# LSTM attention: the softmax numerators turned by four 32-column products with 8 identity columns, in place of one 128x128 transpose

## The reference

```python
def attend(h):
    q = h @ Wq.T
    scores = jnp.einsum('bc,bsc->bs', q, context)
    alpha = jax.nn.softmax(scores, axis=-1)
    ctx = jnp.einsum('bs,bsc->bc', alpha, context)
    return jnp.tanh(jnp.concatenate([ctx, h], axis=-1) @ Wout.T + b_out)

def step(carry, x_t):
    h, c, attn = carry
    inp = jnp.concatenate([x_t, attn], axis=-1)
    gates = inp @ W_ih.T + b_ih + h @ W_hh.T + b_hh
    i, f, g, o = jnp.split(gates, 4, axis=-1)
    c = jax.nn.sigmoid(f) * c + jax.nn.sigmoid(i) * jnp.tanh(g)
    h = jax.nn.sigmoid(o) * jnp.tanh(c)
    out = attn_out = attend(h)
    return ((h, c, attn_out), out)
```

## Time and profile before

| | |
|---|---|
| three timed runs | 6492.47, 6497.38, 6498.66 us; median 6497.38 |
| the profiled execution, its own time | 6499.01 us |
| its span, first to last instruction | 6497.2 us |
| mean granted TensorE clock | 0.966 of full |
| PE busy, share of the span | 89% |
| DVE, ACT busy | 58%, 33% |
| the LSTM loop, first to last transpose on PE | 261.7 to 4528.6 us |

### The profile page before, as it was taken

One profiled execution on the slowest core, in us unless ns is written; L12 is line 12 of the kernel. 1 busy time (PEld: TensorE's weight loads), 2 busy tenths in 40 slices (PEclk: granted clock), 3 DMA queues, 4 the chain that ended last, 5 costly groups with the idle time before them and its releaser, 6 DMA issues. The chain is left out here.

```text
span 6497.2 us, 369971 instructions
## 1 busy us (share of the span) xinstructions
PE 5781.7 (89%) x163920; PEld 3976.9 (61%) x163920; DVE 3736.9 (58%) x16359; ACT 2118.1 (33%) x7992; POOL 290.1 (4%) x779
## 2 busy tenths in 40 slices
PE   6899999999999999999999999999888779795979
PEld 2577777777777777777777777776434334443433
DVE  4355555555555555555555555555387998888852
ACT  3133333333333333333333333333122122222221
POOL 0000000000000000000000000000011011111000
PEclk8999999999999999999999999999898889897989
DMA  1100000000000000000000000000111101010111
GB/s 65 53 2 2 2 2 2 2 2 2 2 2 2 2 2 2 2 2 2 2 2 2 2 2 2 2 2 18 59 39 35 34 21 48 24 55 17 43 31 55
DMA packets 42841, 105.28 MB, mean 16 GB/s; under 512 B 7912, under 2 KB 9960, under 8 KB 42240
## 3 DMA queue, kind: packets, MB, share of 16 engines
q1 hardware_dynamic: 41312, 103.13, 5.2%
q10 hardware_dynamic: 1440, 1.06, 0.1%
HBM read 93.64 MB, written 10.52 MB: 16 GB/s over the span
## 5 line engine op out<-in xcount | busy, mean ns | idle before, releaser
L653 PE MATMUL lstm_part_ps<-lstm_keys,lstm_hid 128*4 128x128 f32 x32768 | 1036.1, 273 | 205.6 <-DVE lstm_hid L804 205.6
L669 PE MATMUL lstm_ctx_ps<-lstm_values,lstm_alpha 128*4 128x128 f32 (+1 forms) x49152 | 1092.6, 237 | 0.0
L653 PEld LDWEIGHTS lstm_part_ps<-lstm_keys,lstm_hid 128*4 128x4 f32 x32768 | 770.4, 86 | 440.2 <-DVE lstm_hid L804 426.0
L669 PEld LDWEIGHTS lstm_ctx_ps<-lstm_values,lstm_alpha 128*4 128x4 f32 x49152 | 895.8, 87 | 94.0
L831 DVE TENSOR_REDUCE lstm_neg_max<-lstm_part_ps 128x1 f32<-128x128 f32 x1024 | 298.4, 291 | 566.3 <-PE lstm_part_ps L653 566.3
L769 ACT ACTIVATE lstm_expo<-lstm_part_ps,lstm_neg_max 128x128 f32<-128x128 f32 x1024 | 376.4, 368 | 749.3 <-DVE lstm_neg_max L831 749.3
L612 PE MATMUL lstm_half_ps<-lstm_w_hid,lstm_hid 128*13 128x96 f32 x16384 | 591.0, 247 | 0.0
L789 DVE STREAM_TRANSPOSE lstm_gates<-lstm_half_ps 128x96 f32<-128x96 f32 x1024 | 289.9, 283 | 433.6 <-PE lstm_half_ps L612 409.5
L612 PE MATMUL lstm_half_ps<-lstm_w_attn,lstm_attn 128*13 128x96 f32 x16416 | 475.5, 247 | 0.7 <-ACT lstm_attn L782 0.7
L776 ACT ACTIVATE lstm_out_row<-lstm_ctx_ps,lstm_factor 128x128 f32<-128x128 f32 x512 | 188.4, 368 | 682.4 <-PE lstm_ctx_ps L669 682.4
L810 DVE COPY lstm_alpha<-lstm_part_ps 128x8 f32<-128x8 f32 x1024 | 176.6, 172 | 382.5 <-PE lstm_part_ps L676 382.5
(11 more groups left out here) (332 smaller groups left out, 8597.5 us busy)
## 6 DMA issues: line engine op xcount, KB each, us to landing
mix_ring<-in_sm_chunks SPq DMA_DIRECT2D x120, 358.0 KB, 3.0
mix_ring<-in_mix_chunks SPq DMA_DIRECT2D x64, 384.0 KB, 3.1
lstm_xg<-xg_rows SPq DMA_DIRECT2D x514, 16.0 KB
xg_rows<-lstm_xg_tile SPq DMA_DIRECT2D x16, 512.0 KB, 2.6
ctxT<-in_ctxT SPq DMA_DIRECT2D x1, 2048.0 KB, 14.8
out_xT<-xT SPq DMA_DIRECT2D x4, 512.0 KB, 3.8
xT<-in_xT SPq DMA_DIRECT2D x1, 1536.0 KB, 9.8
lstm_w_x<-in_lstm_w_x SPq DMA_DIRECT2D x1, 1024.0 KB, 7.8
```

What stands on the lines that cost most here:

```text
L653: mm = pe.matmul(part_rows(score_ps[part], b), hid[:, k, lo:lo + SPACE], keys[:, k, b * SRC + c * P:b * SRC + (c + 1) * P], start=(n == 0 ...
L669: mm = pe.matmul(part_rows(ctx_ps[n], b), alpha[:, b, c, SPACE - 1 - c:2 * SPACE - 1 - c], values[:, b * SC + c, ctx_cols[n]], start=(c == ...
```

## The change

`turn(part)` no longer transposes 128x128. It issues four products, one for each group of 32 positions: the stationary operand is `expo[:, part, 32j:32j+32]` (128 rows, 32 columns), the streamed operand eight columns of the identity, those with the numbers 32b+2*part and 32b+2*part+1, and the output goes to partitions 32j to 32j+31 of a `turned_ps[part]` that is now 8 columns wide. The copy reads these eight adjacent columns in place of a strided choice out of 128. And DVE's second copy is moved behind the two factor sums.

```diff
-            turned_ps = [part_ps[n][:, 2 * P:3 * P] for n in range(PARTS)]
+            turned_ps = [part_ps[n][:, 2 * P:2 * P + 2 * BATCH] for n in range(PARTS)]
...
                 def turn(part):
 
-                    pe.transpose(turned_ps[part], expo[:, part, :], ident[:, :]).then_inc(alpha_turned, 1)
+                    part_columns = ident[:, :].rearrange("p (b r) -> p b r", r=STRIP)[:, :, 2 * part:2 * part + 2]
+                    for j in range(QUARTERS):
+                        mm = pe.matmul(turned_ps[part][j * STRIP:(j + 1) * STRIP, :], expo[:, part, j * STRIP:(j + 1) * STRIP],
+                                       part_columns, start=True, stop=True)
+                    mm.then_inc(alpha_turned, 1)
...
                 def keep_turned(t, part):
                     dve.wait_ge(alpha_turned, 2 * t + part + 1)
-                    turned = turned_ps[part].rearrange("p (b r) -> p b r", r=STRIP)[:, :, 2 * part:2 * part + 2]
+                    turned = turned_ps[part].rearrange("p (b r) -> p b r", r=2)
                     dve.tensor_copy(alpha[:, :, 2 * part:2 * part + 2, SPACE - 1], turned).then_inc(alpha_ready, 1)
...
                         dve.transpose(spread_blocks(spread_total[:, :]), every_row(total[:, :])).then_inc(total_spread, 1)
-                        keep_turned(t, 1)
                         dve.wait_ge(shrink_ready, t + 1)
                         dve.wait_ge(total_spread, t + 1)
                         dve.scalar_tensor_tensor(out=by_part(weighed[:, :]), ...
                         dve.scalar_tensor_tensor(out=own_terms[:, :], ...
+                        keep_turned(t, 1)
                         dve.wait_ge(total_ready, t + 1)
```

## The result

The changed kernel takes 6363.24 us (median of 4 runs, 6359.51 to 6365.27) against 6498.02 us (4 runs, 6492.47 to 6505.70): a ratio of 0.9787, 95% interval 0.9775 to 0.9799 (the two medians alone give 0.9793). It is 134.8 us faster; forecast were 123 (6374 us, range 6340 to 6455). The profiled execution has a span of 6363.5 us and a mean granted clock of 0.966, as before.

The account below looks back on a forecast made before the run. Bound: the closed ring of one loop step, with PE deciding when context(2) starts. After the change DVE's list decides, context(2) comes 0.24 us earlier a step; 512 x 0.24 = 123 us, 6497.4 - 123 = 6374 us, range 6340 to 6455.

Parts of the forecast that it names:

- The ring: Closed chain through one loop step, attention output through scores, turn, context sums and scaling back to attention output; 8.35 us a step.
- The turn's own time: From the turn's first PE load to DVE's copy: 0.33 us instead of 0.37, with ends 0.29 and 0.47.
- one pair at a time: Rival: wide loads on PE don't run beside each other, load to copy 0.47; gain 41 us, 6456 us; chance 0.13.
- the two prices of the Trainium skill: An estimated 27 ns for a 32-column load and 25 ns least per matmul, about 0.2 us for eight.
- The stream around the second turn: PE's 0.40 us loss between context(0) and context(1) shrinks to 0.05 to 0.15; PE free for context(2) 0.36 earlier.
- the gap is not the turn's shape: Rival: the 0.40 around the second turn comes from something that stays; gain 20 us, 6477 us; chance 0.07.
- The second copy: Behind DVE's factor sums it starts at 7.90 or 7.94; alpha at 8.13 or 8.17, 0.11 given back before context(2).
- The sum: context(2) earlier by 0.25 or 0.21 us a step, 0.24 taken; over 512 steps 123 us, giving 6374 us.
- the first turn's L: L is the time from a turn's PE load to DVE's copy; forecast 0.33 us, now 0.37.
- The factor: Ready at 8.45 us, before PE's piece 0 at 8.82 releases the scaling: covered by 0.37.
- At nothing: Terms priced at zero: copying eight adjacent columns, 14 more PE instruction pairs a step; POOL and DMA queues not touched.
- Slower: Rival: 32-column float32 loads as slow as the transpose's 128 and one behind another; 225 us slower, 6722 us; chance 0.04.

Follow-up runs that it names:

- e4: Changed kernel with the four products of a turn made one over the whole array, 8 columns streamed: 6560.3 us, ratio 1.0092 to the kernel before.
- e2: Changed kernel with DVE's second copy back in its old place ahead of the factor sums, four small products kept: 6350.8 us, ratio 0.977 to the kernel before.
- e3: Changed kernel with DVE's transpose that spreads the maxima moved ahead of the first copy: 6354.2 us, ratio 0.9773 to the kernel before.
- e1: Kernel before, 128x128 transpose kept, with only DVE's second copy moved behind the two factor sums: 6500.2 us, ratio 1.000.
- e5: Changed kernel, four column groups kept, but all 128 identity columns streamed in each product: 6504.5 us, ratio 1.0006 to the kernel before.
- e7: e2 with the second turn issued ahead of the last of the three pieces of context(0): 6321.9 us, ratio 0.9723 to the kernel before.
- e8: e2 with four steps unrolled in a round instead of two on every engine: 8048.8 us, ratio 1.2378.
- e6_turn_twice: Changed kernel with the four small products of each turn issued twice: 6421.2 us, ratio 0.9874 to the kernel before.

## Why the prediction was right, point by point

*What bounds the kernel.* The ring through one step bounded it: the loop is 135.1 us shorter by the traces, the kernel 134.8 by the times. PE's busy share stayed at 89%. The loop shows it in both kinds of step: 8.27 to 8.00 inside a round and 8.43 to 8.16 across its branch, 0.27 less in each.

*The turn's own time.* Forecast 0.33 from load to copy, measured 0.32; the ends 0.29 and 0.47 weren't needed. The loads do run beside each other: eight take 0.16 with 110 ns each, so they start 7 ns apart (in the second turn 0.19, 11 ns apart), not 23 to 27. The first turn's eight matmuls take 0.25 at 176 ns each, 11 ns apart. That settles the rival "one pair at a time" and, with it, the two prices of the Trainium skill that spoke for it.

*The stream around the second turn.* Forecast 0.10 from the last matmul of `context(0)` to the first of `context(1)`, measured 0.10. The rival "the gap is not the turn's shape" falls with e4: one whole-array product of 8 columns brings a gap of 0.47 back.

*The second copy.* Forecast: PE free at 8.02, alpha ready at 8.13 or 8.17, a new wait of 0.11. Measured, counted from the first turn's load: alpha ready 1.60 later, forecast 8.13 - 6.52 = 1.61; the wait is 0.10. That the wait is DVE's list and the chain to `shrink` is shown by e2 and e3, each of which removes one link and arrives at the same time. The sum took 0.24 between 0.21 and 0.25; the step gave 0.27 by the timeline and 134.8/512 = 0.263 by the times. What made the sum small is the first turn (0.05 for 0.04) and the weight given to the wide spacing on DVE, which didn't occur: the copy starts 0.17 behind the first sum, two short spacings.

*What was said about the move and didn't hold in size.* The prediction held that in its old place the copy would hardly delay PE, so that moving it cost the 0.11. Its premise, a copy at 7.81, took the first turn's L for the second. In a running stream the copy comes 0.37 behind the first load (e2), because the loads run ahead of matmuls that still have to wait for the stream. The move costs 12 us, not 56: about 0.06 in a step inside a round, and nothing in a step across the branch. And e1 shows the other side: with the slow turn the move is free. So the gain of the change is all in the four products (149 us, e2); the move gives 12 of them back.

*The factor.* Ready at 4.10 + 0.28 = 4.38 with the scaling at 4.74, still released by PE: 0.36 of slack, forecast 0.37.

*At nothing.* The copy takes 0.17 as before, and PE's 14 more pairs a step start 7 to 11 ns apart. Put at nothing rightly.

*A slip.* The rival *Slower* has one stretch at 0.40 in its time and at 0.38 in its threshold. It moves its 6722 by 10 us and nothing else.

## What to carry to other kernels

Where a stream of products in column groups is interrupted by one product over the whole array, look for the gap on both sides of it in the timeline (0.42 here, for an instruction of 0.33). The same result from products in the stream's own form can be cheaper although it is eight times as many instructions, but only if they also stream few columns (e4, e5). When a wait on one engine shrinks, read which list of another engine is late next, and try both to move the late instruction and to start its chain earlier; then issue the producer within the stream ahead of it (e7). Before unrolling a loop, count its instructions: a body that had to be fetched anew in every round cost 1700 us.

## What the runs showed of the hardware that was not expected

A loop body of 1296 PE instructions is fetched once, one of 2592 in every round, at 196 KB a round. It costs 3.3 us a step, of which 2.6 are waits for instructions and 0.66 the longer work at a clock of 0.91 (e8).

The step in which PE passes the round's branch is longer by 0.15 to 0.24 us, and by an amount that changes with the kernel, although the wait that the profile calls issue is 0.33 to 0.35 on the loads in each. Mean length of a step over the whole loop, from one start of the first scaling to the next, in us:

| kernel | inside a round | across the branch |
|---|---|---|
| before | 8.27 | 8.43 |
| changed | 8.00 | 8.16 |
| e2_turn_only | 7.95 | 8.19 |
| e3_spread_first | 7.95 | 8.19 |
| e6_turn_twice | 8.09 | 8.31 |
| e7_turn_inside | 7.91 | 8.09 |

What sets the rest of it is open; no run here took the branch away at an unchanged body.
